# Graph network on one core: running slot counts accumulated in PSUM, and the message stream in five parts instead of seven

## The reference

```
h = relu(layernorm(x))
agg = segment_sum(h[src], dst) / max(count(dst), 1)
x = x + log_softmax(agg @ W_l.T + h @ W_r.T + b)
h = relu(layernorm(x)) @ Wl + bl
weight = relu(edge_attr @ W1 + b1) @ W2 + b2        # one row of 128 for each edge
x = x + segment_sum(h[dst] * weight, src)
```

## Time and profile before

| what | value |
|---|---|
| runs | 3462.42, 3466.47, 3465.89 us; median 3465.89 |
| profiled execution | span 3469.3 us (no time of its own is listed beside it; the median is 3.4 us less) |
| busy in the span | PE 86%, DVE 79%, ACT 60%, POOL 52% |
| TensorE clock, mean granted | 0.959 of full |
| DMA | 593 MB, mean 171 GB/s |

### The profile page before, as it was taken

How to read it: one execution, slowest core, us unless ns; L and a number is a source line. 1 busy time by engine, 2 the same in 40 slices (tenths; PEclk the granted TensorE clock), 3 DMA queues, 4 the chain that set the end, 5 groups by cost and what they waited for, 6 DMA issues and landing times.

```text
span 3469.3 us, 97235 instructions
## 1 busy us (share of the span) xinstructions
PE 2987.6 (86%) x26330; PEld 2437.6 (70%) x26331; DVE 2757.6 (79%) x7718; ACT 2085.3 (60%) x4907; POOL 1808.5 (52%) x1790
## 2 busy tenths in 40 slices
PE   0799999999668878899999989988889898998977
PEld 0699999999655556776766666766667666766766
DVE  8899999999786657777777777777777777777866
ACT  2599999998353335555555545555455555555656
POOL 3400010000127777667766676666766677677750
PEclk9999999999868889999999999999999999999999
DMA  3198888960103336666666656655666666666657
GB/s 117 37 326 313 311 309 310 311 213 3 38 19 107 103 103 172 179 175 160 178 164 161 160 150 172 166 162 147 166 168 180 165 158 184 173 158 175 181 154 207
DMA packets 506188, 593.04 MB, mean 171 GB/s; under 512 B 71050, under 2 KB 477058, under 8 KB 505905
## 3 DMA queue, kind: packets, MB, share of 16 engines
q1 hardware_dynamic: 449506, 470.49, 49.4%
q0 software_dynamic: 56400, 119.07, 9.9%
HBM read 293.94 MB, written 295.35 MB: 170 GB/s over the span
## 4 chain that ended last, share of the span: by engine, by line
DVE 36%; PE 32%; issue 17%; DVEq 7%; DMA 4%; POOL 2%; ACT 1%; SPq 0%; POOLq 0%; ACTq 0%
PE PS L1119 11%; DVE X L1017 8%; PE PS L1110 5%; DVE big L990 4%; PE PS L1282 4%; PE PS L1249 4%; DMA messages<-big,idxr 4%; DVE big L978 3%; DVE aux L768 3%; DVEq L1012 3%; DVE big L964 2%; DVE big L975 2%; DVE big L967 2%; DVE hpar L1006 2%; PE PS L1261 2%
## 5 line engine op out<-in xcount | busy, mean ns | idle before, releaser
L605 POOL DMA_INDIRECT messages<-big,idxr x1664 | 1637.0, 984 | 720.8 <-issue 466.5
L1282 PE MATMUL PS<-big,hpar 128*128 128x128 f32 x5120 | 663.8, 283 | 163.7 <-DVE hpar L1006 128.7
L1282 PEld LDWEIGHTS PS<-big,hpar 128*128 128x128 f32 x5120 | 610.5, 195 | 223.1 <-DVE hpar L1006 181.2
L1432 ACT ACTIVATE big<-PS,b1c 128x512 f32<-128x512 f32 x416 | 286.0, 688 | 708.3 <-PE PS L1238 708.3
L1017 DVE TENSOR_TENSOR X<-X,PS 128x128 f32 x1280 | 368.7, 288 | 325.3 <-PE PS L1282 131.9
L1119 PE MATMUL PS<-h_parts,counts 128*128 128x258 f32 x3626 | 565.3, 296 | 0.0
L1359 ACT ACTIVATE counts<-PS 128x784 fp32r<-128x784 f32 x592 | 481.7, 825 | 93.9 <-PE PS L1110 85.6
L1249 PE MATMUL PS<-W2s,big 128*128 128x128 f32 x3328 | 500.8, 295 | 0.0
L1249 PEld LDWEIGHTS PS<-W2s,big 128*128 128x128 f32 x3328 | 419.0, 197 | 98.3 <-issue 98.3
L1119 PEld LDWEIGHTS PS<-h_parts,counts 128*128 128x128 f32 x3626 | 470.2, 191 | 0.2 <-ACT counts L1359 0.2
L1443 ACT ACTIVATE big<-PS 128x512 f32<-128x512 f32 x416 | 247.6, 595 | 347.2 <-PE PS L1261 339.4
(11 more groups left out here) (222 smaller groups left out, 3639.1 us busy)
## 6 DMA issues: line engine op xcount, KB each, us to landing
messages<-zeros SPq DMA_DIRECT2D x896, 193.5 KB
big<-messages SPq DMA_DIRECT2D x320, 516.0 KB
aux<-slot_rows SPq DMA_DIRECT2D x416, 128.0 KB
big<-in_edge_attr_dram SPq DMA_DIRECT2D x402, 128.0 KB
messages<-big,idxr POOLq DMA_INDIRECT x1664
X<-in_x_dram SPq DMA_DIRECT2D x12, 448.0 KB, 6.9
out_dram<-X SPq DMA_DIRECT2D x6, 448.0 KB
edge_places<-big SPq DMA_DIRECT2D x1, 2496.0 KB, 13.2
```

Of the source, the lines that this page charges most:

```text
L605: pool.indirect_dma_start(strm_d, bass.IndirectOffsetOnAxis(ap=idxr[:, n % U, j:j + 1], axis=0), outr[:, n % U, j, :], None).then_inc(S_sc ...
L1282: last = nc.tensor.matmul(to[:, r * C:(r + 1) * C], finhot[:, n % 2, r * 2 + q, :], fin[:, k, r, q * ROW:q * ROW + C], start=(q == 0), sto ...
```

## The change

1. **Counts in PSUM.** The tile `pQ` in PSUM is no longer opened anew for each group. It is opened once for each part with the first rows of the blocks (`starts`), and each group's `ranks` adds what came since: the rest of the tile before (`upto`, the complement of `tri`), the whole tiles between (`onesb`, three times), and the slots ahead in the same tile (`tri`). That is five matmuls of 200 columns in place of one of 250 and one of 200; where the ring of one-hots wraps, once in eight groups, the three become six pieces. DVE loses the running sums over tiles, `taken` and its update, the add of `taken`, and the cast: `own_places` multiplies `pQ` by the one-hot, and `row_places` reduces straight into `idxr`. `ranks` of a group must now wait until `own_places` of the group before has read `pQ`. The one-hots get a ring of eight groups (`RING`).
2. **Five parts.** `LOOPS` has five entries, all with two rings, so each round has eight groups (before: sixteen, or eight in three of the loops). `EVERY` names all later loops. The first part has 141 groups (before 53). There are 284 octs, 244 in steps and 40 in the tail; 172 steps have none. The written-out stretches of 12 steps fall from six to four.
3. **Order on DVE.** The adds of the oct of the step before stand one by one between the other operations, the first at the head of the step; `own_places` and `row_places` stand ahead of `messages`, `one_hot_T` stands last, and the load of the block registers stands ahead of `messages`.
4. Slots without a block get rows of their own for each part behind the stream, which are not zeroed; SP zeroes 758 slices of the stream instead of 896. `block_signs` makes five activations in a half instead of seven.

In the built programs a round of the looped octs has 604 instructions on DVE and 889 on PE in the longest loop of before (sixteen groups), 304 and 447 in its loops of eight groups, and 259 and 466 in the changed kernel.

```diff
-    LOOPS = ((3, 4), (5, 2), (4, 4), (4, 4), (3, 4), (5, 2), (2, 2))
-    EVERY = (1, 4, 5, 6)
+    LOOPS = ((17, 2), (10, 2), (7, 2), (6, 2), (3, 2))
+    EVERY = (1, 2, 3, 4)
...
             def block_hot(g, n):
-                s = n % 2
-                wait(dve, S["rank_done"], g - 1)
-                nc.vector.tensor_tensor(hotW[:, s, 1:, :], iotaB[:, :].unsqueeze(1).to_broadcast([P, J, NBK]),
+                at = n % RING * J
+
+                wait(dve, S["rank_done"], g - RING + 2)
+                nc.vector.tensor_tensor(hotW[:, at:at + J, :], iotaB[:, :].unsqueeze(1).to_broadcast([P, J, NBK]),
                                         blcol[:, 0, ds(g * J, J)].unsqueeze(2).to_broadcast([P, J, NBK]), ALU.is_equal).then_inc(S["hot_ready"], 1)
-                dve.wait_ge(S["hot_ready"], g * 3 + 1)
-                nc.vector.tensor_tensor(hotU[:, 2:, :], hotW[:, s, 1:, :], hotW[:, s, 0:J, :], ALU.add).then_inc(S["hot_ready"], 1)
-                dve.wait_ge(S["hot_ready"], g * 3 + 2)
-                nc.vector.tensor_tensor(hotV[:, s, 1:, :], hotU[:, 2:, :], hotU[:, 0:J, :], ALU.add).then_inc(S["hot_ready"], 1)
+
+            def own_places(g, n):
+                at = n % RING * J
+                dve.wait_ge(S["rank_done"], g + 1)
+                wait(dve, S["rank_chain"], g * 2)
+                nc.vector.tensor_tensor(place, pQ, hotW[:, at:at + J, :], ALU.mult).then_inc(S["rank_chain"], 1)
...
+                k = n % U
+                dve.wait_ge(S["rank_chain"], g * 2 + 1)
                 wait(dve, S_sc[k], (g - k) * 16)
-                nc.vector.tensor_copy(idxr[:, k, :], place_f).then_inc(S["rank_chain"], 1)
+                with nc.allow_low_precision(reason="one term of each sum is not zero"):
+                    nc.vector.tensor_reduce(idxr[:, k, :], place, AX, ALU.add).then_inc(S["rank_chain"], 1)
...
+                add(0)
                 if not isinstance(s, int) or s + 2 < G:
                     block_hot(s + 2, n + 2)
+                add(1)
+                if o:
+                    stream_hot(*o)
+                add(2)
+                if more:
+                    own_places(s + 1, n + 1)
+                add(3)
+                if more:
+                    row_places(s + 1, n + 1)
+                if o:
+                    pair_places(o[0])
+                messages(s, n)
                 if more:
                     one_hot_T(s + 1, n + 1)
-                if o:
-                    stream_hot(*o)
-                messages(s, n)
-                if more:
-                    row_places(s + 1, n + 1)
-                if adding[0]:
-                    block_adds(o[0] - 1 if o else adding[0][0], pFL[adding[0][1] % 2])
...
             def ranks(g, n):
-                pe.wait_ge(S["hot_ready"], g * 3 + 3)
-                wait(pe, S["rank_chain"], g * 5)
-                nc.tensor.matmul(pQ, onesb[:, :], hotV[:, n % 2, :, :], start=True, stop=False)
-                nc.tensor.matmul(pQ[:, 0:J, :], tri[:, :], hotW[:, n % 2, 1:, :], start=False, stop=True).then_inc(S["rank_done"], 1)
+                at = n % RING * J
+                pe.wait_ge(S["hot_ready"], g + 1)
+                wait(pe, S["rank_chain"], g * 2 - 1)
...
+                elif at:
+                    counted(upto, 0, at - J, J)
+                    for k in range(1, J):
+                        counted(onesb, 0, at - J + k, J)
...
+                nc.tensor.matmul(pQ, tri[:, :], hotW[:, at:at + J, :], start=False, stop=True, skip_group_check=True).then_inc(S["rank_done"], 1)
```

More of the change, by code:

```diff
@@ L55, in gnn_program @@
     NOCT = sum(OCTS)
-    CAP = NOCT * FO + P
-    CAP += -CAP % 3
-    assert all(o * FO >= n + 2 * NB for o, n in zip(OCTS, SLOTS)) and (CAP - NOCT * FO) * P >= NS * P - E
+    BIN = -(-(NS * P - E) // P)
+    ZF = NOCT * FO + -NOCT * FO % 3
+    CAP = ZF + NPART * BIN
+    assert all(o * FO >= n + 2 * NB for o, n in zip(OCTS, SLOTS))
     NPAIR = NOCT * FO // 2
@@ L63, in gnn_program @@
     NO_NODE = 30000
-    IR = 6
+    RING = 8
     D = 2
@@ L827, in split_starts @@
             def split_starts():
-                nc.vector.tensor_copy(starts[:, 0, NB:], starts[:, NPART - 1, NB:])
+                for p in range(NPART):
+                    last = nc.vector.memset(starts[:, p, NB:], float((ZF + p * BIN) * P))
+                last.then_inc(S["starts_ready"], 1)
                 link(nc.vector.tensor_copy(split, starts[:, 0, 1:NB]))
@@ L949, in _ @@
             dve.wait_ge(S["z_done"], NCH)
-            nc.vector.memset(hotW, 0.0)
-            nc.vector.memset(hotU, 0.0)
-            nc.vector.memset(hotV, 0.0)
-            link(nc.vector.tensor_copy(taken, starts[:, 0, :]))
             def one_hot_T(g, n):
@@ L995, in _ @@
             block_hot(1, 1)
+            own_places(0, 0)
             row_places(0, 0)
@@ L1009, in stream_hot, with pair_places, block_add @@
                                         ALU.is_equal).then_inc(S["finhot_ready"], 1)
[L1011 to L1018 removed]
+            def pair_places(i):
+                dve.load(pair_regs, bq_i[0:1, ds(i * (FO // 2), FO // 2)])
+            def block_add(i, r, sums):
+                at = dve.snap(pair_regs[r], min_val=0, max_val=(NB - 1) * C)
+                dve.wait_ge(S["finmm_done"], i + 1)
+                wait(dve, S["fadd_done"], i * (FO // 2) + r)
+                nc.vector.tensor_tensor(Xf[:, ds(at, C)], Xf[:, ds(at, C)], sums[:, r * C:(r + 1) * C], ALU.add).then_inc(S["fadd_done"], 1)
+            def block_adds(i, sums):
+                pair_places(i)
+                for r in range(FO // 2):
+                    block_add(i, r, sums)
             adding = [None]
@@ L1045, in _ @@
             steps(dve, layer1, next_part)
-            block_adds(OCT0[-1] - 1, pFL[(OCT0[-1] - 1) % 2])
+            for r in range(FO // 2):
+                block_add(OCT0[-1] - 1, r, pFL[(OCT0[-1] - 1) % 2])
             def segment(i, n):
@@ L1265, in ranks, with counted @@
             def ranks(g, n):
-                pe.wait_ge(S["hot_ready"], g * 3 + 3)
-                wait(pe, S["rank_chain"], g * 5)
-                nc.tensor.matmul(pQ, onesb[:, :], hotV[:, n % 2, :, :], start=True, stop=False)
-                nc.tensor.matmul(pQ[:, 0:J, :], tri[:, :], hotW[:, n % 2, 1:, :], start=False, stop=True).then_inc(S["rank_done"], 1)
+                at = n % RING * J
+                pe.wait_ge(S["hot_ready"], g + 1)
+                wait(pe, S["rank_chain"], g * 2 - 1)
+                opens = FIRST.index(g) if isinstance(g, int) and g in FIRST else None
+                def counted(before, j, t, tiles):
+                    nc.tensor.matmul(pQ[:, j:j + tiles, :], before[:, :], hotW[:, t:t + tiles, :], start=False, stop=False, skip_group_check=True)
+                if opens is not None:
+                    nc.tensor.matmul(pQ, ident[:, :], starts[:, opens, :].unsqueeze(1).to_broadcast([P, J, NBK]), start=True, stop=False,
+                                     skip_group_check=True)
+                    for k in range(1, J):
+                        counted(onesb, J - k, at, k)
+                elif at:
+                    counted(upto, 0, at - J, J)
+                    for k in range(1, J):
+                        counted(onesb, 0, at - J + k, J)
+                else:
+                    counted(upto, 0, (RING - 1) * J, J)
+                    for k in range(1, J):
+                        counted(onesb, 0, (RING - 1) * J + k, J - k)
+                        counted(onesb, J - k, 0, k)
+                nc.tensor.matmul(pQ, tri[:, :], hotW[:, at:at + J, :], start=False, stop=True, skip_group_check=True).then_inc(S["rank_done"], 1)
             attr_T(0, 0)
```

56 lines of the change are left out of this document (20 added, 36 removed).

## The result

The changed kernel takes 3322.53 us, the median of 4 runs (3319.26 to 3328.24), beside 3464.15 us (4 runs, 3461.38 to 3466.47) for the kernel before in the same comparison: a ratio of 0.9592, 95% interval 0.9577 to 0.9606. The forecast was 3341.5 us in a range of 3290 to 3420. The profiled execution after has a span of 3317.3 us and a time of 3319.26 us.

A forecast was written before the change was run, and what follows sets the result against it. It took DVE to bound the oct steps, PE close behind, and POOL the steps without octs. Stage -129.1, tail +9.7, ahead of the steps -1.6 and -3.4 sum to -124.4: median 3465.9 becomes 3341.5 us, range 3290 to 3420.

The forecast's parts named there:

- The bound moves from DVE to PE: Oct steps: DVE needs about 4.65 us and is ready first, so PE becomes the bound; chance 0.61.
- The register load: DVE's load of block registers in oct steps: expected covered by work queued ahead of it; uncovered it adds 0.67 us.
- The size of the step: Looped oct steps on PE: 5.15 + 0.26 + 0.02 + 0.04 = 5.47 us, against 5.97 before.
- Without the wait PE would take 5.93 - 0.78 = 5.15 us: PE's own pace in an oct step of the kernel before, without its wait for DVE's one-hots of the oct.
- The first part: The first 140 intervals, without octs, stay at POOL's pace of 5.08 us a group: 706 us.
- The rival of the starved stretch: First part: late `one_hot_T` and low clock put PE at 5.47 us, above POOL's 5.08; 55 us more, 3396; chance 0.11.
- The written-out stretches: Four stretches of 12 steps in the message stage at 59.2 us each, 236.8 in all.
- DVE's slack: Oct steps: DVE is ready before PE's next `node_rows`, with 0.1 to 0.8 us to spare.
- Round ends: Ends of eight-group rounds cost PE 0.04 us a step, 0.3 an end; the six pieces perhaps 0.02 a group.
- the slower rival: Code stalls at all 43 round ends, about 5 us each: +200, 3542 us; it decides from 2.9 an end; chance 0.04.
- Tail and stretches ahead: Tail: four more octs at 2.42 us, +9.7; ahead of the steps: layer 0 -1.6 and the table stretch -3.4.
- the -1.6: Layer 0: two of seven activations go, 64 halves x 0.09 x 2/7 = -1.6 us, between 0 and -5.8.

The follow-up runs named there:

- experiment 4: Changed kernel with two more matmuls of 200 columns in every `ranks`, into PSUM that nothing reads: 3369.71 us.
- Experiment 3: Changed kernel with DVE's old order: the four adds together at the end, `one_hot_T` behind `block_hot`, `messages` ahead of the places: 3308.41 us.
- experiment 9: Changed kernel with `one_hot_T` of the next group ahead of `block_hot` again, behind the first add, the adds still spread: 3322.38 us.
- experiment 2: Changed kernel with the old table (seven parts, rounds of sixteen groups in three loops), counts in PSUM and new order kept: 3349.36 us.
- 12: Experiment 9's kernel with `messages` of a group also moved ahead of `own_places` and `row_places` of the next: 3320.88 us.
- 8: Changed kernel with DVE adding up one-hots of three tiles, so `ranks` has three matmuls instead of five, and DVE's old order: 3290.30 us.
- 10: Changed kernel with DVE adding up one-hots of three tiles (three matmuls in `ranks`) and `one_hot_T` ahead of `block_hot`: 3292.06 us.

## Why the prediction was right, point by point

**The bound moves from DVE to PE: right.** The oct steps show no PE wait for DVE, DVE waits for the sums, and experiment 4 lengthens the step by the matmuls it adds. Experiment 3 shows that it is the shorter DVE step, not its new order, that brings this. The register load is covered, as forecast.

**The size of the step: 5.33, not 5.47.** The matmuls were priced well: from `ranks` to the bias product 0.53 us against 0.29 + 0.26 = 0.55, and +0.085 a matmul. Too high was "Without the wait PE would take 5.93 - 0.78 = 5.15 us". That took away the wait ahead of the sums but kept the 1.88 us from the sums to `node_rows` of a step that had waited. In the step after, the first weight load of the sums starts at 2803.57, under the transposes, and it is 1.79; without the new matmuls PE's own step is 5.30 - 0.24 = 5.06. The matmuls cost 0.24, forecast 0.26; the ends of rounds and the wrap 0.04, forecast 0.06. Together that is the 0.14 between 5.47 and 5.33: over 208 steps 30 us, more than the whole miss of 24 in the stage.

**The first part: right in its sum, 706.8, for partly another reason.** POOL never paused. The rival of the starved stretch put PE at 5.47 there at a low clock; PE needs 5.05 and the clock rose from 0.84 to 0.98, so the low clock with which that rival reckoned did not come. Its mechanism was real, though: the late one-hot does stretch PE's step, to a hair of POOL's group. That POOL still set the pace there was luck as much as reckoning.

**The written-out stretches: mis-sized by 8 us.** I took 59.2 for all four from one stretch of the kernel before. The first, behind the part without octs, takes 64.3, in the old order of experiment 3 as well, and that alone is 5.1 of the 8 us. In it DVE's head start on POOL shrinks, from 6.1 us at group 139 to 3.4 at group 151 (11.5 to 8.8 in experiment 3), where it grows in the later ones; why is open. The later three could have been shorter than forecast: with the lag worked off in a loop DVE can run ahead of POOL, and they take 55 us in experiment 3. The new order keeps them at 60, first by the late one-hot, which I had followed for the first part and not here, and behind it, as experiment 9 shows, by `row_places`, whose wait for POOL now stands ahead of `messages` and which I did not follow.

**DVE's slack: right in size by luck.** "0.1 to 0.8 us to spare" holds the 0.4 measured, but two errors cancel in it. I counted to the start of `node_rows`, and to there DVE has 1.41 us on average, since its step is shorter than my 4.65: 3.54 us from the end of the sums to the end of `one_hot_T` (the steady step above: 2803.88, 3.41 behind the start of the first add, which starts 0.13 behind the sums). And I left out that the addresses that the products need are computed behind the same wait, which takes about 1 us of that away. The forecast of the step did not suffer, since some room was left.

**Round ends: right in time, wrong on the engine.** Ends of eight groups and the wrap cost 0.04 a step, 0.3 a round; the slower rival needed 2.9, and sixteen groups have 6.5. The prediction had DVE's body of 604 instructions stall. The traces show DVE's branch at most 0.07 us long, in the kernel before too; what waits is PE's branch. In the kernel before it takes 4.0 to 5.4 us at six of the eight ends of sixteen groups with octs that go round again, in experiment 2 3.7 to 4.1 at five of eight, and nowhere over 0.24 at ends of eight groups. So the length of the body is not all that decides, and what else does is open. The rule that stood beside that rival (the Trainium skill, "Runtime: NRT & Kernel Launch", Instruction fetch mechanics: a branch out of the loaded pages waits for a fetch) agrees in that a branch can wait; that it is a fetch it waits for no run here shows.

**Tail and stretches ahead: right in sign**, +8.8 for +9.7 and -7.5 for -5.0. Layer 0 with counting runs at (795.2 - 407.9) / 37 = 10.47 a half, as before, so the -1.6 for it is not seen:

```profile
L775 DVE TENSOR_REDUCE aggv<-PS x38: 423/424/426, 407.9 to 795.2; 128x128 f32<-128x256 f32 x38
```

The wait behind layer 0 accounts for 2.9 of the -7.5 (11.8 to 8.9, forecast 3.4). The rest is no proof of a saving: kernels with the same code ahead of the stage start it anywhere from 1032.3 to 1041.1.

**What stays open.** Experiment 3 beats the changed kernel by 14 us; 12 explains the head start and the first part, not why POOL catches up in the loops under the old order alone. The runs to settle it were not made. The best versions are 8 and 10, 3290 and 3292 us, with POOL's group at 5.15 and 5.17 us in the first oct loop beside steps of 5.18: there POOL is close to being the bound everywhere, and the next gain probably has to come from it.

## What to carry to other kernels

When a wait on the path goes, take the engine's own pace from a step that did not wait, from end to end: what hides under the neighbouring work changes with it. An engine that idles ahead of its next wait is not slack by that much: look at what the waiting side still has to do behind the same semaphore, register arithmetic among it. And when instructions are reordered on an engine, follow each wait that is moved ahead of another instruction, the ones for a slow engine's buffers above all: they decide how far the fast engines can run ahead.

## What the hardware showed that I had not expected

**A scatter of POOL waits out a DVE operation.** In the changed kernel's loop, from 1830 to 2200, 62 of 277 scatters last over 1.0 us, 1.24 on average where the others take 0.96, and three start late; all 65 are the second of a group and meet `stream_hot`. One place:

```profile
1837.65 0.96 POOL L603 DMA_INDIRECT messages<-big,idxr  x1 [0.30 <-issue]
...
1838.94 0.68 DVE L998 TENSOR_TENSOR hpar<-iotaN,big 128x512 f32<-128x512 f32 x1
...
1839.60 0.96 POOL L603 DMA_INDIRECT messages<-big,idxr  x1 [0.99 <-issue]
```

The next scatter was due at 1838.91, 0.30 after the one before ended at 1838.61; it starts at 1839.60, as `stream_hot` ends at 1839.62. In the steady step above one is as late, due at 2801.46 and held to 2802.14, though `stream_hot` (2801.15 to 2801.83) has ended 0.31 before. Of the 63 scatters that start while `stream_hot` runs, 62 are the long ones; of the 45 that start while `messages` runs, which reads one of its inputs from PSUM, none is. The Trainium skill ("SBUF — State Buffer", SBUF: two separate sides) says that VectorE and GpSimd share a pair of SBUF ports as an exclusive lock, which a VectorE operation with two SBUF inputs takes against a GpSimd operation that reads SBUF. `stream_hot` has two such inputs, and the trace agrees: it is this operation that delays the scatter, by 0.7 us at both places. In groups 170 to 230 three of the four spacings have a median of 1.263 us and the one behind a group's second scatter 1.51: POOL goes from group to group without a pause and still takes 5.3 us, PE's step, where 4 x 1.263 makes 5.05.

**The clock in the steps without octs** does not follow from PE's busy time alone. From 1054 to 1304 it was 0.84 with 203.2 us busy of 250 before, 0.90 in experiment 9 with 197.3 and 0.84 in experiment 10 with 199.5. It was 0.98 after with 237.2, where the products of `node_rows` are drawn out over 1.65 us by the address arithmetic and count as busy in between. What sets it apart in 9 and 10 is open.
